# DVE convolves the first x block of a step before it multiplies the next decays with B*C

## The reference, cut to what matters

```python
xn = layernorm(x)                                    # x: 4 sequences x 256 tokens x 512
proj = xn @ in_proj_w.T
gate, xBC, dt = split(proj)                          # 8192, 8192 + 2*8*128, 128
xBC = silu(depthwise_conv(xBC, conv_w, K=4) + conv_b)
x, B, C = split(xBC)                                 # 128 heads of 64; B, C: 8 groups of 128
dt = clip(softplus(dt + dt_bias), 0.001, 100)
cs = cumsum(dt * A)                                  # over time; A = -1 ... -128
y = ((C @ B.T) * exp(cs_l - cs_s), s <= l) @ (x * dt) + D * x
yg = y * silu(gate)                                  # then rms norm within each of 8 groups
s = (yg * rstd * norm_w) @ out_proj_w.T
g = silu(top-2-of-16 expert FFN(xn))
out = x_in + s * g
```

## Time and profile before

| | |
|---|---|
| time, median of 3 runs | 1604.44 us |
| profiled execution, its own time | 1603.83 us |
| its span | 1602.0 us |
| busy: PE, DVE, ACT, POOL | 99%, 88%, 75%, 60% |
| granted clock of TensorE | 0.999 |
| one group in the loop (910.0 to 1090.5) | 180.5 us, PE busy 180.33, DVE 164.11 |

### The profile page before, as it was taken

How to read it: one execution, slowest core, us unless ns; L and a number is a source line. 1 busy time by engine, 2 the same in 40 slices (tenths; PEclk the granted TensorE clock), 3 DMA queues, 4 the chain that set the end, 5 groups by cost and what they waited for, 6 DMA issues and landing times.

```text
span 1602.0 us, 28468 instructions
## 1 busy us (share of the span) xinstructions
PE 1587.9 (99%) x8478; PEld 1266.6 (79%) x8478; DVE 1406.6 (88%) x1654; ACT 1199.9 (75%) x2309; POOL 959.6 (60%) x600
## 2 busy tenths in 40 slices
PE   9999999999999999999999999999999999999998
PEld 6888777887778777887778777887778777877776
DVE  7727899889999899889999899889998899889987
ACT  5525878777787878777787878777887878778772
POOL 6522466655666656655666556655666566656563
PEclk9999999999999999999999999999999999999999
DMA  5234344334443344334443334334433334334432
GB/s 188 80 131 150 127 138 169 115 132 142 146 146 112 128 137 165 118 131 143 141 146 117 127 130 168 122 130 144 145 141 119 126 129 166 126 120 152 152 132 86
DMA packets 83832, 216.89 MB, mean 135 GB/s; under 512 B 10576, under 2 KB 12880, under 8 KB 83536
## 3 DMA queue, kind: packets, MB, share of 16 engines
q1 hardware_dynamic: 83376, 214.55, 39.3%
q10 hardware_dynamic: 288, 0.30, 0.1%
HBM read 209.83 MB, written 4.98 MB: 134 GB/s over the span
## 4 chain that ended last, share of the span: by engine, by line
PE 84%; DVE 7%; ACT 4%; issue 3%; POOL 1%; DMA 0%; ACTq 0%; DVEq 0%; POOLq 0%
PE pj L455 15%; PE pj L457 14%; PE pj L456 14%; PE pr L455 9%; PE pr L456 8%; PE pr L457 7%; PE sc L702 7%; PE sc L706 3%; PE tb L691 3%; DVE conv L1394 3%; ACT decay L984 1%; DVE decay L1422 1%; DVE xc L1408 1%; DVE wo_lo L1458 1%; PE pr L680 1%
## 5 line engine op out<-in xcount | busy, mean ns | idle before, releaser
L1096 POOL TENSOR_TENSOR w_lo<-stg,w_hi 128x512 fp32r<-128x512 f32 x316 | 494.9, 1567 | 315.1 <-ACT w_hi L958 254.4
L455 PE MATMUL pj<-xT_hi,w_hi 128*128 128x512 f32 x1208 | 476.5, 394 | 3.6 <-POOL w_lo L1096 1.5
L457 PE MATMUL pj<-xT_hi,w_lo 128*128 128x512 f32 x1208 | 470.8, 390 | 0.0
L456 PE MATMUL pj<-xT_lo,w_hi 128*128 128x512 f32 x1208 | 470.4, 389 | 0.0
L1394 DVE SCALAR_TENSOR_TENSOR conv<-pj,par,conv 128x510 f32<-128x510 f32 (+2 forms) x480 | 357.8, 745 | 77.0 <-ACT conv L966 63.6
L984 ACT ACTIVATE decay<-decay,dtg 128x256 f32<-128x256 f32 (+1 forms) x1024 | 379.0, 442 | 0.0
L1137 POOL TENSOR_TENSOR xc<-xc,thg 128x512 f32<-128x512 f32 x128 | 203.1, 1587 | 188.9 <-DVE xc L1445 188.6
L1143 POOL TENSOR_TENSOR sqsum<-sqsum,sq 128x512 f32<-128x512 f32 x112 | 216.7, 1935 | 115.4 <-ACT sq L1012 112.1
L455 PEld LDWEIGHTS pj<-xT_hi,w_hi 128*128 128x128 f32 x1208 | 226.7, 188 | 58.8 <-issue 8.5
L457 PEld LDWEIGHTS pj<-xT_hi,w_lo 128*128 128x128 f32 x1208 | 226.7, 188 | 48.2
L456 PEld LDWEIGHTS pj<-xT_lo,w_hi 128*128 128x128 f32 x1208 | 226.9, 188 | 45.3
(11 more groups left out here) (185 smaller groups left out, 1976.4 us busy)
## 6 DMA issues: line engine op xcount, KB each, us to landing
stg<-wstream SPq DMA_DIRECT2D x387, 256.0 KB, 2.7
decay<-cs_scr SPq DMA_DIRECT2D x128, 768.0 KB, 4.3
acc<-hid SPq DMA_DIRECT2D x8, 256.0 KB, 5.0
out<-acc SPq DMA_DIRECT2D x8, 256.0 KB, 2.0
dt_scr<-decay SPq DMA_DIRECT2D x1, 1024.0 KB, 5.7
gate_scr<-part SPq DMA_DIRECT2D x4, 256.0 KB, 2.0
dtg<-dt_scr SPq DMA_DIRECT2D x16, 64.0 KB, 4.1
stg<-hid SPq DMA_DIRECT2D x4, 256.0 KB, 4.9
```

What stands on the lines that cost most here:

```text
L455: nc.tensor.matmul(dst, hi_w, hi_x, start=first, stop=False)
L456: nc.tensor.matmul(dst, hi_w, lo_x, start=False, stop=False)
L457: return nc.tensor.matmul(dst, lo_w, hi_x, start=False, stop=last)
L1096: nc.gpsimd.tensor_tensor(w_dest(n, 1), stg[:, s % RING, :], f32(w_dest(n, 0)), ALU.subtract).then_inc(S["wl"], 1)
```

## The change

In `step` of the vector block the taps of the first x block now always come ahead of `block_weights`; before, they did so in the fill alone.

```diff
-                fill = isinstance(g, int) and g < 0
-                if fill and mine:
+                if mine:
                     taps(g, half, mine[0])
                 if has_pair(g, half, s + 1):
                     block_weights(*pair(g, half, s + 1))
-                if mine and not fill:
-                    taps(g, half, mine[0])
```

## The result

The new order took 1629.49 us (median of 4, 1628.65 to 1634.77) against 1605.26 us for the order of before on the same chip: a ratio of 1.0156, 95% interval 1.0143 to 1.017. The forecast was 1619.5, range 1611 to 1625. The profiled execution has a span of 1626.9 us, 24.9 more than before.

What follows compares the result with a forecast made beforehand. PE's busy time was taken as the bound, so only added PE waits count: 13.6 (step 6) + 0.7 (square sums) + 0.8 (group 0) + 0.1 (group 7) = 15.2 us, giving a median of 1619.6 us, range 1611 to 1625.

Steps and rivals of the forecast that it cites:

- The order and its first cost: Step 5 of half 0: DVE already waits for ACT's tap, so the product comes wholly behind it, adding 1.67 us.
- The path to step 4: Half 0: delay of 0.82 us from step 3 makes the second x block's taps in step 4 0.63 us later.
- gate_silu at step 6: Half 0, groups 1 to 6: gate_silu 2.3 us later holds up PE's second x block; 13.6 us after slack.
- nothing of half 1 stalls: Half 1: delays of 1.7 to 2.4 us end in DVE's waits and 3.1 us of slack at step 6.
- I take it as a fixed cost of the turn: ACT's gap at its loop's jump back, ahead of step 5: stays 2.65 to 2.86 us, passing on the 0.63 delay.
- between 0 (the gap shrinks by 0.63) and all of it: Bounds on how much of the 0.63 us delay passes through ACT's turn; the forecast took all.
- the square sums: Step 1 of half 1: PE waits 0.1 us for DVE's x times dt to free a bank, seven groups, 0.7 us.
- group 0: First group, without ACT's gap and with DVE late since the start: about +0.8 us.
- group 7: Last group, without ACT's gap and with room for PE's second x block: +0.1 us.
- The turn did take part: Rival: ACT's gap absorbs the 0.63 us, only 1.67 reaches step 6; 1616 us, chance 0.09.
- The product met no w_lo: Rival: product meets POOL's w_lo in half 0 steps 4 and 5, up to 1.3 us more; 1627 us, chance 0.05.
- The loop through POOL and ACT: Rival: later x times D delays POOL's gating, ACT's y_hi and next tap; half 1 stalls; 1634 us, chance 0.03.

Runs made afterwards that it cites:

- Experiment 4: 768 KB exponents' load of half 0 step 5 issued one weight load later: new order 1617.97 us, order of before 1605.2, new order with PE's loop written out 1623.67.
- experiment 2: New order with one engine's loop over the groups written out, so it has no jump back: ACT's 1609.16 us, PE's 1639.67 us.
- experiment 3: New order with SP issuing the 768 KB exponents' load ahead of the weight loads in half 0: step 4 1646.43 us, steps 3 and 4 1639.43 us.

## Why the prediction was off

- **The order and its first cost: right.** The product comes wholly behind ACT's tap in step 5 and is 1.75 us there (960.60). By itself it moves the span by 10.8 us; 10.0 was worked out.
- **The path to step 4: right.** The second taps end 0.58 later against PE's stream in group 4 (0.63 was worked out): their start is 0.82 us ahead of the start of PE's last matmul of the step (946.26) now, 1.40 before (932.67). gate_silu at step 6 is the releaser, nothing of half 1 stalls, the product's mean is 1758 ns (1760 foretold). ACT's x tanh waits 138.9 us for DVE instead of 174.1, as foretold.
- **The step that failed: "I take it as a fixed cost of the turn".** That the gap had been 2.65 to 2.86 us "whenever ACT reached it" was true of turns that all stood alike towards the 768 KB load, so it was one case seen six times and not a bound. The bounds I set, "between 0 (the gap shrinks by 0.63) and all of it", left out that the gap could grow. A shift of 0.6 us put the read behind the load: +7.0 us. Experiment 4 shows it: with this load issued later, and the tanh as late as without that edit, the gap is 2.51 us and the growth is gone. This is the larger part of the miss (24.9 - 15.2 = 9.7 us in the spans).
- **Left out: the clock behind PE's waits.** I had asked who waits how long, not what PE does afterwards. 4.1 us; with the 7.0 this is 11.1, against which stand 0.7 for the square sums, which never waited (they start 0.23 us behind the matmul ahead of them in all 16 places, before and after, so the bank that I had them wait for had been free in time), 0.5 in group 0 and 0.1 in group 7. That these stand against the 11.1 is luck: without them the miss would be larger still.
- **Missed without harm here: PE's own turn.** It is hidden in the chain of ACT in the kernel after, but it is what is left when ACT's turn is taken away (experiment 2). I wrote "no DMA and no wait" of the change, but SP's ring waits for DVE's wo_lo (L1458), which comes 0.8 us later from step 3 on. SP issues the exponents' load of step 4 6.33 us ahead of PE's last matmul of the step now (939.93 and 946.26) and 7.14 before (925.53 and 932.67); its last packet begins 1.3 to 2.8 us ahead of that matmul now and 2.4 to 3.9 before, and a weight load and then PE's read follow it (the read 0.7 to 1.4 us ahead now, 1.7 to 2.8 before). That PE's gap hangs on this load too is borne out by experiment 3, where it went with the load, but there other things had changed; it isn't shown by a run of its own.
- **The rivals.** The turn did take part, but the other way round. The product met no w_lo. The loop through POOL and ACT did not close, though ACT's y_hi (tile yT_hi) now waits for POOL 46 times (40.7 us; once, 3.1 us, before).

## What to carry to other kernels

A gap that recurs with one size is not a constant until one knows what it waits for: look at what else is in flight beside it, the DMA queues' own instruction reads among it, and ask what stands next to it when one side moves and the other does not. An order between engines that is nearly tied (here a load issued 0.3 us ahead of a jump back, whose read came when at most 5 of the load's 128 packets had begun) deserves a bound on both sides. And a wait of TensorE costs more than its length when its clock falls behind it, so a sum of waits is a lower end where single waits reach the 2.3 us behind which it first fell here.
